# The W stage of a LoRA and routed-adapter kernel: another order of the weight pieces, a first piece in two transfers, PT in five parts over two queues

## The chip, the cores and the metric

One core of a Trainium2 chip (trn2) runs the kernel. The metric is the time on the device in microseconds, the median of several executions of the same program.

## The reference

```python
# x (8, 512, 2048), W (2048, 2048), lora_As (32, 2048, 16), lora_Bs (32, 16, 2048), all float32
base_out = jnp.einsum('bti,oi->bto', x, W) + b
lora_h   = jnp.einsum('bti,bir->btr', x, lora_As[adapter_mapping])      # one adapter per batch
lora_out = jnp.einsum('btr,bro->bto', lora_h, lora_Bs[adapter_mapping])
cond     = base_out + lora_out * 2
logits   = jnp.einsum('bsd,ed->bse', cond, route_w)                     # 8 experts, the top one
route_weight = one_hot(argmax(logits)) * max(logits)
h        = jnp.einsum('bsd,erd->bser', cond, A)                         # (8 experts x rank 16)
out      = x + jnp.einsum('bser,eor->bso', route_weight[..., None] * h, Bw)
```

The result `cond` is needed only in two products, with `A` and with `route_w`. So the kernel never makes it. It multiplies the weights together first and then works on x with the small product.

## The kernel before

The rows of `A` (128) and of `route_w` (8) stand beside each other as PT, 136 columns, cut into 16 chunks of 128 output features of W. All arrays are laid out so by the host.

**W stage.** It computes M = W^T PT, 2048 x 136. W comes in 32 pieces of 512 KB: 8 blocks of 256 input features (`NWB`), each in 4 parts along the output features (`NWH`), with 4 chunks to a part. A piece is 8 matmuls of 136 columns in float32, and the profile records each of them as two. SP loads the pieces into a ring of 8 (`w_ring`); from the ninth on it waits until PE has used the slot (L211). Pieces go block after block: block 0 parts 0 to 3, then block 1, and so on. A block has two accumulators, both in one of two double banks of PSUM (`bank_out`), used in turn. PT comes in 4 parts, each issued by SP just before one of the first four W pieces (L228 to L232); behind piece 4 SP issues the bias.

When a block is complete (`t_w` counts the pieces that PE has finished), ACT copies it from PSUM: the 128 columns rounded to `m_hi`, and the 8 routing columns twice to `ext`. DVE then subtracts to get the rest `m_lo` (`m_block` in each). The semaphore `v_m` counts DVE's lots, and PE waits for it before it writes the bank again (L502).

ACT's program during this stage is one loop over the 8 blocks. In the pass for block 1, ahead of that block's eviction and behind block 0's, it issues the eight loads of loraB (one adapter for each batch, 128 KB each) and two of loraA (L320 to L324); the rows' numbers were read much earlier. POOL waits for all eight, rearranges them into `lb_cols` and signals `g_lb` (L283, L284).

**The side products.** PE's program is written out in order: warm-up matmuls (L513 to L515), W pieces 0 to 19, then a wait for `g_lb` and the product of the loraB columns with PT (L519 to L523), the bias product (L527, which needs the chain of 16 operations in DVE over PT and the bias, L395 to L399), pieces 20 to 23, small products (L533, L536), pieces 24 to 31.

**The rest.** Then come eight batches of 512 tokens, the last in two halves. For each, PE computes the LoRA and routing product (L573), the main product in three passes of split float32 (L588 to L590), the routing (L598, L604, L615), and the output products of the batch before (L555 to L557). DVE adds x to them, and SP stores. x comes in 32 pieces of 1 MB; SP issues the first four within the W stage, behind pieces 19, 23, 27 and 31, and BwT (1 MB) behind piece 19 too.

Of the kernel before, what the change touches and what calls it, by code (L numbers as in the profile page):

```python
# [41 lines left out]
P = 128  # L42
# [4 lines left out]
def adaln_ffn(nc, xT, slot_of, W, PT, bias, loraA, loraB, BwT, outT):  # L47
    NB, NQ, _, PC, T = xT.shape
    C = NQ * PC
    NP2 = C // 2  # L50
    NWB, NWH, _, WO, WI = W.shape
    E = 8
    R = 16
    ER = E * R
    PN = ER + E
# [3 lines left out]
    BIAS_ROW = E + R  # L59
    XRING = 12  # L60
    WRING = 8
    NPT = 4
    SRING = 4
    NWP = NWB * NWH
    NPIECES = NB * NQ
    assert ER == P and WI == 2 * P and NWB == NP2 and NB * R == P and BIAS_ROW < GROUP

    ctx = ExitStack()
    with ctx:
# [6 lines left out]
        def sem(name):  # L76
            return ctx.enter_context(nc.semaphore(name))
# [3 lines left out]
        w_ring = sb("w_ring", [P, WRING, WO, WI], F32, phase1)  # L81
# [15 lines left out]
        pt = sb("pt", [P, C, PN], F32, phase1)  # L97
# [14 lines left out]
        m_hi = sb("m_hi", [P, C, ER], F32R)  # L112
# [34 lines left out]

        d_slots, d_bias, d_bw, d_lb, d_la0, d_la = (sem(n) for n in ("d_slots", "d_bias", "d_bw", "d_lb", "d_la0", "d_la"))
        d_pt = [sem(f"d_pt{i}") for i in range(NPT)]
        d_w = [sem(f"d_w{i}") for i in range(WRING)]  # L150
        d_x = [sem(f"d_x{i}") for i in range(XRING)]
        d_out = [sem(f"d_out{i}") for i in range(XRING)]
# [28 lines left out]
            return x_ring[:, k % XRING, 2 * j % PC:2 * j % PC + 2, t0:t0 + nt]  # L181

        CONSTS = E + 7
        WARM_UP = 9
        BW_AT = 19
        BP_AT, G_AT = 20, 24

        CHOOSE_AT, EHI_AT, ELO_AT = 1, 5, 3

        def out_banks(u, j):  # L190

# [15 lines left out]
        @block.sync  # L207
        def _(sp):
            def load_w(n):
                if n >= WRING:  # L210
                    sp.wait_ge(t_w, n - WRING + 1)  # L211
                sp.dma_start(w_ring[:, n % WRING, :, :], W[n // NWH, n % NWH]).then_inc(d_w[n % WRING], 16)

            def load_x(k):
                slot = k % XRING
                if k >= XRING:
                    sp.wait_ge(d_out[slot], 16 * (k // XRING))
                elif slot in EARLY:
                    sp.wait_ge(t_g, len(g_banks))
                    sp.wait_ge(v_bw, 1)  # L220
                sp.dma_start(x_ring[:, slot, :, :], xT[k // NQ, k % NQ]).then_inc(d_x[slot], 16)

            def store(k):
                sp.wait_ge(v_out, (k + 1) * (PC // 2))
                sp.dma_start(outT[k // NQ, k % NQ], x_ring[:, k % XRING, :, :]).then_inc(d_out[k % XRING], 16)


            for n in range(NWP):  # L228
                if n < NPT:
                    part = slice(n * C // NPT, (n + 1) * C // NPT)  # L230
                    sp.dma_start(pt[:, part, :], PT[:, part, :]).then_inc(d_pt[n], 16)
                load_w(n)  # L232
                if n == NPT:
                    sp.dma_start(bias_sb[:, :], bias).then_inc(d_bias, 16)
                if n == BW_AT:
                    sp.dma_start(bw_raw, BwT).then_inc(d_bw, 16)
                if n >= NWP - 4 * NQ and n % 4 == 3:
                    load_x((n - NWP + 4 * NQ) // 4)
            for k in range(NQ, XRING):
                load_x(k)  # L240
            LAG = 2
            LAST = NPIECES - NQ
            for k in range(LAST):
                store(k)
                if k >= LAG and k - LAG + XRING < NPIECES:
                    load_x(k - LAG + XRING)
            for u in range(NB - 1, NU):
                b, t0, nt = UNITS[u]
                for j in range(NP2):
                    sp.wait_ge(v_out, NP2 * u + j + 1)  # L250
                    q, c = 2 * j // PC, 2 * j % PC
                    sp.dma_start(outT[b, q, :, c:c + 2, t0:t0 + nt], x_pair(u, j)).then_inc(d_last, 16)
            for s in range(XRING):
                sp.wait_ge(d_out[s], 16 * len(range(s, LAST, XRING)))
            sp.wait_ge(d_last, 16 * NP2 * (NU - NB + 1))
# [39 lines left out]
        @block.scalar  # L295
        def _(act):

            act.dma_start(slots[:, :], slot_of).then_inc(d_slots, 16)
            act.wait_ge(d_slots, 16)
            slot = [act.value_load(slots[0:1, b:b + 1], min_val=0, max_val=NSLOTS - 1) for b in range(NB)]  # L300
# [7 lines left out]
            def copy(out, in_, done):  # L308
                act.activation(out, in_, ACT.Copy).then_inc(done, 1)  # L309

            def m_block(n):

                act.wait_ge(t_w, NWH * (n + 1))
                copy(m_hi[:, 2 * n:2 * n + 2, :], bank_out[n % 2][:, :, 0:ER], a_m)
                for i in range(2):
                    copy(ext[i][:, 2 * n:2 * n + 2, 0:E], bank_out[n % 2][:, :, ER:PN], a_m)

            act.wait_ge(g_const, CONSTS)
            for n in range(NWB):
# [60 lines left out]
        def _(dve):  # L380
            def sub(out, a, b, done):
                dve.tensor_tensor(out, a, b, ALU.subtract).then_inc(done, 1)  # L382

            def m_block(n):
                dve.wait_ge(a_m, 3 * (n + 1))
                sub(m_lo[:, 2 * n:2 * n + 2, :], bank_out[n % 2][:, :, 0:ER], m_hi[:, 2 * n:2 * n + 2, :], v_m)

            dve.memset(warm[:, :], 0.0).then_inc(v_warm, 1)

            dve.wait_ge(d_bias, 16)  # L390
            for c in range(C):
                if c % (C // NPT) == 0:
                    dve.wait_ge(d_pt[c // (C // NPT)], 16)
                if c == 0:
                    dve.tensor_scalar(pb_sum[0][:, :], pt[:, 0, :], bias_sb[:, 0:1], None, ALU.mult).then_inc(v_pb, 1)  # L395
                else:
                    dve.wait_ge(v_pb, c)
                    dve.scalar_tensor_tensor(out=pb_sum[c % 2][:, :], in0=pt[:, c, :], scalar=bias_sb[:, c:c + 1],
                                             in1=pb_sum[(c - 1) % 2][:, :], op0=ALU.mult, op1=ALU.add).then_inc(v_pb, 1)  # L399
# [94 lines left out]
        def _(pe):  # L494
            mm = pe.matmul

            def w_piece(n):

                blk, half = divmod(n, NWH)
                pe.wait_ge(d_w[n % WRING], 16 * (n // WRING + 1))  # L500
                if half == 0 and blk >= 2:
                    pe.wait_ge(v_m, blk - 1)  # L502
                for i in range(2):
                    for o in range(WO):
                        k = half * WO + o
                        if blk == 0 and i == 0 and k % (C // NPT) == 0:
                            pe.wait_ge(d_pt[k // (C // NPT)], 16)
                        last = mm(bank_out[blk % 2][:, i, 0:PN], w_ring[:, n % WRING, o, i * P:(i + 1) * P],  # L508
                                  pt[:, k, :], start=(k == 0), stop=(k == C - 1))
                last.then_inc(t_w, 1)  # L510


# [4 lines left out]
                w_piece(n)  # L517

            pe.wait_ge(g_lb, 1)  # L519
            for c in range(C):  # L520
                last = mm(bank_l[:, 0:PN], lb_cols[:, c, :, :].rearrange("p b r -> p (b r)"), pt[:, c, :],  # L521
                          start=(c == 0), stop=(c == C - 1))
# [18 lines left out]
            def out_pair(u, j):  # L541
                nt = UNITS[u][2]
                if u == 0 and j < 2:
                    pe.wait_ge(v_m, NWB)
                else:
                    pe.wait_ge(v_out, pairs_added(u, j))
                if u == 0 and j == 0:
                    pe.wait_ge(v_bw, 1)
                if j == 0:
                    pe.wait_ge(v_whlo, u + 1)  # L550
                hi, lo = wh_hi[u % 2][:, 0:nt], wh_lo[u % 2][:, 0:nt]
                for i in range(2):
                    o = slice((2 * j + i) * P, (2 * j + i + 1) * P)
                    out = out_banks(u, j)[:, i, :]
                    mm(out, bw_hi[:, o], hi, start=True, stop=False)  # L555
                    mm(out, bw_hi[:, o], lo, start=False, stop=False)  # L556
                    last = mm(out, bw_lo[:, o], hi, start=False, stop=True)  # L557
                last.then_inc(t_out, 1)

            pe.wait_ge(v_glo, 1)  # L560
            for u, (b, _, nt) in enumerate(UNITS):
# [4 lines left out]
                for r in range(C // NGROUPS):  # L566
                    for g in range(NGROUPS):
                        c = r * NGROUPS + g
                        if c % PC == 0:
                            x_landed(pe, NQ * b + c // PC)  # L570
                        if u == 0 and c % 2 == 0:
                            pe.wait_ge(a_m, 3 * (c // 2 + 1))
                        last = mm(bank_e[g * GROUP:(g + 1) * GROUP, 0:nt], ext[u % 2][:, c, :], x_pair(u, c // 2)[:, c % 2, :],  # L573
                                  start=(r == 0), stop=(r == C // NGROUPS - 1))
                last.then_inc(t_ext, 1)

                if u >= 1:
                    pe.wait_ge(a_h, u)
                else:
                    pe.wait_ge(v_m, NWB)  # L580
                h = bank_h[:, 0:nt]
                for j in range(NP2):
                    g = NP2 * u + j
# [71 lines left out]
```

## Time and profile before

| | us |
|---|---|
| median of 3 runs | 304.76 |
| lowest, highest | 304.1, 304.79 |
| span of the profiled execution | 302.6 |
| the profiled execution's own time on the device | not given beside its span |
| TensorE (PE) busy, matmul | 295.9 |
| VectorE (DVE) busy | 193.1 |
| ScalarE (ACT) busy | 99.0 |
| GpSimd (POOL) busy | 11.0 |

The span runs from the first to the last instruction of one execution. Busy time is the time in which an engine's rows lie, idle time the rest. PEld is TensorE's weight load, which overlaps its matmuls. Queues of DMA issues have a q behind the engine's name. The chain of waits is followed from the last instruction back to what released it, step by step. The granted clock (PEclk) of 1.00 stands for 2.4 GHz.

### The profile page before, as it was taken

Reading aid. Unit: us, or ns where it says so; the run is one execution under the profiler, and the core shown is the slowest. Engines: PE = TensorE matmul, PEld = TensorE weight load, DVE = VectorE, ACT = ScalarE, POOL = GpSimd, SP = SyncE. Lnnn points to the kernel's source line nnn. Section 1 sums busy time; section 2 is a strip of 40 time slices with the busy share of each in tenths; the row PEclk is TensorE's granted clock in tenths of the full one; section 3 lists DMA queues with packets and bytes.
Section 4 is the critical chain, followed back from the end, with each engine's and each line's share of the span. In section 5 each row is a group of like instructions: output and inputs, shape, how many; then the busy total and the mean of one; then the engine's idle time right before and its main releaser. Section 6 shows DMA issues by size and latency. Waiting matters only on the chain.

```text
span 302.6 us, 4629 instructions
## 1 busy us (share of the span) xinstructions
PE 295.9 (98%) x1857; PEld 233.5 (77%) x1857; DVE 193.1 (64%) x258; ACT 99.0 (33%) x147; POOL 11.0 (4%) x37
## 2 busy tenths in 40 slices
PE   7899999999999999999999999999999999999994
PEld 4899999997675885788488758866884787787994
DVE  0160000242894997498579839984985796698775
ACT  0020000223874332534253433424342533322410
POOL 6000300000100000000000000000000000000000
PEclk9999999999999999999999999999999999999999
DMA  7999999999920067739946991998399569536468
GB/s 245 400 404 394 415 412 411 414 417 418 421 107 2 25 252 259 298 133 388 418 172 237 417 405 54 379 395 337 118 377 417 202 220 406 208 151 266 178 218 299
DMA packets 20790, 88.44 MB, mean 292 GB/s; under 512 B 2210, under 2 KB 8354, under 8 KB 12962
## 3 DMA queue, kind: packets, MB, share of 16 engines
q1 hardware_dynamic: 18464, 86.06, 72.4%
q10 hardware_dynamic: 2306, 2.10, 2.0%
q8 instruction: 14, 0.23, 0.3%
q14 instruction: 6, 0.05, 0.0%
HBM read 54.60 MB, written 33.55 MB: 291 GB/s over the span
## 4 chain that ended last, share of the span: by engine, by line
PE 92%; DMA 3%; DVE 3%; SPq 1%; issue 0%
PE bank_out L508 18%; PE bank_h L588 11%; PE bank_h L590 10%; PE bank_h L589 10%; PE bank_e L573 9%; PE bank_out L555 9%; PE bank_out L557 9%; PE bank_out L556 9%; DMA w_ring<-W 3%; DVE x_ring L465 2%; PE bank_l L521 1%; PE bank_r L615 1%; PE bank_l L598 1%; PE bank_h L608 1%; PE bank_h L610 1%; PE bank_h L609 1%
## 5 line engine op out<-in xcount | busy, mean ns | idle before, releaser
L382 DVE TENSOR_TENSOR x_lo<-x_ring,x_hi 128x1024 fp32r<-128x1024 f32 (+1 forms) x72 | 78.9, 1106 | 41.1 <-ACT x_hi L309 41.1
L309 ACT ACTIVATE x_hi<-x_ring 128x1024 fp32r<-128x1024 f32 (+1 forms) x72 | 69.2, 966 | 85.8 <-PE bank_h L590 85.8
L465 DVE TENSOR_TENSOR x_ring<-bank_out,x_ring 128x1024 f32<-128x1024 f32 (+1 forms) x72 | 79.2, 1102 | 1.4 <-PE bank_out L557 1.1
L508 PE MATMUL bank_out<-pt,w_ring 128*128 128x136 f32 x512 | 60.6, 280 | 1.4 <-DMA w_ring<-W 1.4
L508 PEld LDWEIGHTS bank_out<-pt,w_ring 128*128 128x128 f32 x512 | 59.7, 190 | 2.8 <-DMA w_ring<-W 2.5
L588 PE MATMUL bank_h<-x_hi,m_hi 128*128 128x512 f32 (+1 forms) x144 | 55.1, 383 | 0.0
L555 PE MATMUL bank_out<-wh_hi,bw_hi 128*128 128x512 f32 (+1 forms) x144 | 54.6, 379 | 0.0
L590 PE MATMUL bank_h<-x_hi,m_lo 128*128 128x512 f32 (+1 forms) x144 | 53.3, 370 | 0.0
L556 PE MATMUL bank_out<-wh_lo,bw_hi 128*128 128x512 f32 (+1 forms) x144 | 53.2, 369 | 0.0
L557 PE MATMUL bank_out<-wh_hi,bw_lo 128*128 128x512 f32 (+1 forms) x144 | 53.2, 369 | 0.0
L589 PE MATMUL bank_h<-x_lo,m_hi 128*128 128x512 f32 (+1 forms) x144 | 53.1, 369 | 0.0
L588 PEld LDWEIGHTS bank_h<-x_hi,m_hi 128*128 128x128 f32 x144 | 27.0, 188 | 13.2 <-issue 8.5
L590 PEld LDWEIGHTS bank_h<-x_hi,m_lo 128*128 128x128 f32 x144 | 27.1, 188 | 5.0
L557 PEld LDWEIGHTS bank_out<-wh_hi,bw_lo 128*128 128x128 f32 x144 | 27.1, 188 | 5.0
L555 PEld LDWEIGHTS bank_out<-wh_hi,bw_hi 128*128 128x128 f32 x144 | 27.1, 188 | 4.8
L589 PEld LDWEIGHTS bank_h<-x_lo,m_hi 128*128 128x128 f32 x144 | 27.1, 188 | 4.6
L382 DVE TENSOR_TENSOR m_lo<-bank_out,m_hi 128x256 fp32r<-128x256 f32 x8 | 3.4, 424 | 42.5 <-ACT ext L309 42.5
L556 PEld LDWEIGHTS bank_out<-wh_lo,bw_hi 128*128 128x128 f32 x144 | 27.1, 188 | 4.2
L573 PE MATMUL bank_e<-x_ring,ext 128*32 128x512 f32 (+1 forms) x288 | 29.4, 548 | 0.0
L573 PEld LDWEIGHTS bank_e<-x_ring,ext 128*32 128x32 f32 x288 | 8.4, 109 | 16.4 <-issue 15.3
L309 ACT ACTIVATE m_hi<-bank_out 128x256 fp32r<-128x256 f32 x8 | 3.1, 383 | 44.4 <-PE bank_out L508 44.4
L356 ACT ACTIVATE e_sb<-bank_e,e_bias 128x512 f32<-128x512 f32 (+1 forms) x9 | 5.8, 642 | 25.9 <-PE bank_e L573 25.9
(77 smaller groups left out, 130.1 us busy)
## 6 DMA issues: line engine op xcount, KB each, us to landing
x_ring<-xT SPq DMA_DIRECT2D x32, 1024.0 KB, 9.0
outT<-x_ring SPq DMA_DIRECT2D x28, 1024.0 KB, 5.3
w_ring<-W SPq DMA_DIRECT2D x32, 512.0 KB, 9.0
outT<-x_ring SPq DMA_DIRECT2D x16, 256.0 KB, 2.4
pt<-PT SPq DMA_DIRECT2D x4, 272.0 KB, 5.8
x_ring<-loraB ACTq DMA_DIRECT2D x8, 128.0 KB, 10.6
la<-loraA ACTq DMA_DIRECT2D x8, 128.0 KB, 14.3
x_ring<-BwT SPq DMA_DIRECT2D x1, 1024.0 KB, 10.4
```

What stands on the lines that cost most here:

```text
L309: act.activation(out, in_, ACT.Copy).then_inc(done, 1)
L356: act.activation(e_sb[:, 0:nt], bank_e[:, 0:nt], ACT.Identity, bias=e_bias[:, 0:1]).then_inc(a_e, 1)
L382: dve.tensor_tensor(out, a, b, ALU.subtract).then_inc(done, 1)
L465: dve.tensor_tensor(x, out_banks(u, j), x, ALU.add).then_inc(v_out, 1)
L508: last = mm(bank_out[blk % 2][:, i, 0:PN], w_ring[:, n % WRING, o, i * P:(i + 1) * P], pt[:, k, :], start=(k == 0), stop=(k == C - 1))
L555: mm(out, bw_hi[:, o], hi, start=True, stop=False)
L556: mm(out, bw_hi[:, o], lo, start=False, stop=False)
L557: last = mm(out, bw_lo[:, o], hi, start=False, stop=True)
L573: last = mm(bank_e[g * GROUP:(g + 1) * GROUP, 0:nt], ext[u % 2][:, c, :], x_pair(u, c // 2)[:, c % 2, :], start=(r == 0), stop=(r == C // ...
L588: mm(h, m_hi[:, c, :], hi, start=(c == 0), stop=False)
L589: mm(h, m_hi[:, c, :], lo, start=False, stop=False)
L590: last = mm(h, m_lo[:, c, :], hi, start=False, stop=False)
```

## The change

The order of the W pieces is a list now. The first 16 pieces are the parts 0 of blocks 0 to 3, then their parts 1, and so on; pieces 16 to 31 are blocks 4 to 7 one after the other, as before. Four blocks are open at once, so block 2 accumulates in `bank_e` and `bank_h` and block 3 in `bank_r` and `bank_l`; these two are drained in two lots each, which makes 10 lots. Piece 0 comes in two transfers of two chunks each. PT comes in five parts (2, 2, 4, 4, 4 chunks), the first two issued by ACT ahead of all else, the other three by SP behind pieces 1, 3 and 5. The bias is issued behind piece 7. PE does 6 warm-up matmuls. ACT's and DVE's `m_block` wait for the piece that completes the block, and PE waits before L521 for the drain of the first four blocks. ACT's loop around `m_block` is as before.

```diff
+    PT_PARTS = [(0, 2), (2, 4), (4, 8), (8, 12), (12, 16)]
+    NPT = len(PT_PARTS)
+    OPEN = NWB // 2
+    ORDER = [(blk, part) for part in range(NWH) for blk in range(OPEN)] + [
+        (blk, part) for blk in range(OPEN, NWB) for part in range(NWH)]
+    DONE = [max(n for n in range(NWP) if ORDER[n][0] == blk) + 1 for blk in range(NWB)]
...
-        WARM_UP = 9
+        WARM_UP = 6
...
+        def w_banks(blk):
+
+            if blk == 2:
+                return [(bank_e, 4, 1), (bank_h, 5, 1)]
+            if blk == 3:
+                return [(bank_r, 6, 1), (bank_l, 7, 1)]
+            return [(bank_out[blk % 2], 2 * blk, 2)]
+
+        M_LOTS = [sum(len(w_banks(b)) for b in range(blk + 1)) for blk in range(NWB)]
...
-                sp.dma_start(w_ring[:, n % WRING, :, :], W[n // NWH, n % NWH]).then_inc(d_w[n % WRING], 16)
+                blk, part = ORDER[n]
+                if n == 0:
+                    sp.dma_start(w_ring[:, 0, 0:WO // 2, :], W[blk, part, :, 0:WO // 2, :]).then_inc(d_w_first, 16)
+                    sp.dma_start(w_ring[:, 0, WO // 2:WO, :], W[blk, part, :, WO // 2:WO, :]).then_inc(d_w[0], 16)
+                else:
+                    sp.dma_start(w_ring[:, n % WRING, :, :], W[blk, part]).then_inc(d_w[n % WRING], 16)
...
             for n in range(NWP):
-                if n < NPT:
-                    part = slice(n * C // NPT, (n + 1) * C // NPT)
-                    sp.dma_start(pt[:, part, :], PT[:, part, :]).then_inc(d_pt[n], 16)
                 load_w(n)
-                if n == NPT:
+                if n in (1, 3, 5):
+                    k = 2 + n // 2
+                    c0, c1 = PT_PARTS[k]
+                    sp.dma_start(pt[:, c0:c1, :], PT[:, c0:c1, :]).then_inc(d_pt[k], 16)
+                if n == 7:
                     sp.dma_start(bias_sb[:, :], bias).then_inc(d_bias, 16)
...
         def _(act):
 
+            for k in range(2):
+                c0, c1 = PT_PARTS[k]
+                act.dma_start(pt[:, c0:c1, :], PT[:, c0:c1, :]).then_inc(d_pt[k], 16)
             act.dma_start(slots[:, :], slot_of).then_inc(d_slots, 16)
...
             def m_block(n):
 
-                act.wait_ge(t_w, NWH * (n + 1))
-                copy(m_hi[:, 2 * n:2 * n + 2, :], bank_out[n % 2][:, :, 0:ER], a_m)
-                for i in range(2):
-                    copy(ext[i][:, 2 * n:2 * n + 2, 0:E], bank_out[n % 2][:, :, ER:PN], a_m)
+                act.wait_ge(t_w, DONE[n])
+                for bank, c, k in w_banks(n):
+                    sums = bank[:, :, 0:PN] if k == 2 else bank[:, 0:PN].unsqueeze(1)
+                    copy(m_hi[:, c:c + k, :], sums[:, :, 0:ER], a_m)
+                    for i in range(2):
+                        copy(ext[i][:, c:c + k, 0:E], sums[:, :, ER:PN], a_m)
...
-                blk, half = divmod(n, NWH)
-                pe.wait_ge(d_w[n % WRING], 16 * (n // WRING + 1))
-                if half == 0 and blk >= 2:
-                    pe.wait_ge(v_m, blk - 1)
...
+                blk, part = ORDER[n]
+                if part == 0 and blk >= OPEN:
+                    pe.wait_ge(v_m, M_LOTS[blk - OPEN if blk < OPEN + 2 else blk - 2])
+                halves = ((0, WO // 2), (WO // 2, WO)) if n == 0 else ((0, WO),)
...
             pe.wait_ge(g_lb, 1)
+            pe.wait_ge(v_m, M_LOTS[OPEN - 1])
```

DVE's `m_block` and the later waits for evicted blocks count in lots in the same way.

## Rows read from the trace of the kernel before

**Rows 1.** The page: busy time and share per engine, then the chain of waits.

```profile
PE 295.9 (98%) x1857; PEld 233.5 (77%) x1857; DVE 193.1 (64%) x258; ACT 99.0 (33%) x147; POOL 11.0 (4%) x37
...
PE 92%; DMA 3%; DVE 3%; SPq 1%; issue 0%
PE bank_out L508 18%; PE bank_h L588 11%; PE bank_h L590 10%; PE bank_h L589 10%; PE bank_e L573 9%; PE bank_out L555 9%; PE bank_out L557 9%; PE bank_out L556 9%; DMA w_ring<-W 3%; DVE x_ring L465 2%; PE bank_l L521 1%; PE bank_r L615 1%; PE bank_l L598 1%; PE bank_h L608 1%; PE bank_h L610 1%; PE bank_h L609 1%
```

**Rows 2.** Timeline of PE: start us, length us, line, operation, records, idle before.

```profile
1.19 3.87 PE L515 MATMUL bank_h<-warm 128*128 128x512 bf16 x9 [1.19 <-DVE warm L388]
4.97 2.12 PE L508 MATMUL bank_out<-pt,w_ring 128*128 128x136 f32 x16
8.29 4.06 PE L508 MATMUL bank_out<-pt,w_ring 128*128 128x136 f32 x32 [1.20 <-DMA w_ring<-W]
12.57 31.77 PE L508 MATMUL bank_out<-pt,w_ring 128*128 128x136 f32 x272 [0.23 <-DMA w_ring<-W]
44.18 3.87 PE L521 MATMUL bank_l<-pt,x_ring 128*128 128x136 f32 x32
```

**Rows 3.** Windows of the opening: length, busy per engine, granted clock, DMA share, GB/s.

```profile
0.00:4.00 4.00, 2.81 (x7) 1.01 (x8) 0.27 (x1) 0.00 (x0) 3.44 (x22) 1.00 0.55 182
4.00:8.00 4.00, 3.09 (x19) 2.07 (x17) 0.00 (x0) 0.00 (x0) 1.36 (x6) 1.00 0.98 324
8.00:12.00 4.00, 3.71 (x31) 3.69 (x32) 0.00 (x0) 0.00 (x0) 0.00 (x0) 1.00 1.01 390
12.00:16.00 4.00, 3.77 (x32) 3.57 (x32) 1.73 (x5) 1.22 (x1) 0.00 (x0) 1.00 1.02 412
```

**Rows 4.** Timeline of ACT and its DMA queue (ACTq), around block 0's eviction.

```profile
14.78 1.28 ACT L309 ACT_TABLE_LOAD   x1 [14.78 <-PE bank_out L508]
15.04 0.88 ACTq L322 DMA_DIRECT2D x_ring<-loraB  x2
16.07 0.38 ACT L309 ACTIVATE m_hi<-bank_out 128x256 fp32r<-128x256 f32 x1
...
16.57 3.34 ACTq L322 DMA_DIRECT2D x_ring<-loraB  x5
20.00 0.88 ACTq L304 DMA_DIRECT2D la<-loraA  x2
```

**Rows 5.** The loraB loads' line: issues, and times to landing.

```profile
L322 ACTq DMA_DIRECT2D x_ring<-loraB x8: 339/340/1322, 15.0 to 19.6; - x8
...
DMA to landing us min/median/max: 6.6/10.6/13.7
```

**Rows 6.** Timeline of POOL: the copy that makes the loraB columns.

```profile
33.29 1.89 POOL L284 COPY x_ring<-x_ring 128x2048 f32<-128x2048 f32 x1 [27.93 <-DMA x_ring<-loraB]
```

**Rows 7.** Timeline of SP's DMA queue: issues of W, BwT and x.

```profile
1.19 0.42 SPq L212 DMA_DIRECT2D w_ring<-W  x1
...
29.92 0.43 SPq L236 DMA_DIRECT2D x_ring<-BwT  x1
30.40 0.44 SPq L221 DMA_DIRECT2D x_ring<-xT  x1
```

**Rows 8.** DMA queues, q1 of SP, q10 of ACT: 20 to 33, then 63 to 74 us.

```profile
q1 hardware_dynamic: 1123, 4.10, 80.1%
q10 hardware_dynamic: 1125, 1.02, 23.3%
...
q1 hardware_dynamic: 556, 4.07, 88.3%
q10 hardware_dynamic: 558, 0.51, 13.5%
```

**Rows 9.** Windows at the end of the trace.

```profile
298.00:300.00 2.00, 0.51 (x5) 0.30 (x3) 1.22 (x2) 0.00 (x0) 0.00 (x0) 1.00 1.04 347
300.00:302.00 2.00, 0.00 (x0) 0.00 (x0) 0.00 (x0) 0.00 (x0) 0.00 (x0) 0.94 0.86 286
302.00:302.60 0.60, 0.00 (x0) 0.00 (x0) 0.00 (x0) 0.00 (x0) 0.00 (x0) 0.50 0.00 0
```

More of the change, by code:

```diff
@@ L61, in adaln_ffn @@
     WRING = 8
-    NPT = 4
     SRING = 4
     NWP = NWB * NWH
+    PT_PARTS = [(0, 2), (2, 4), (4, 8), (8, 12), (12, 16)]
[4 more added lines that the diff above has]
+    DONE = [max(n for n in range(NWP) if ORDER[n][0] == blk) + 1 for blk in range(NWB)]
     NPIECES = NB * NQ
@@ L149, in adaln_ffn @@
         d_pt = [sem(f"d_pt{i}") for i in range(NPT)]
+        d_w_first = sem("d_w_first")
         d_w = [sem(f"d_w{i}") for i in range(WRING)]
@@ L384, in m_block @@
             def m_block(n):
-                dve.wait_ge(a_m, 3 * (n + 1))
-                sub(m_lo[:, 2 * n:2 * n + 2, :], bank_out[n % 2][:, :, 0:ER], m_hi[:, 2 * n:2 * n + 2, :], v_m)
+                for i, (bank, c, k) in enumerate(w_banks(n)):
+                    sums = bank[:, :, 0:PN] if k == 2 else bank[:, 0:PN].unsqueeze(1)
+                    dve.wait_ge(a_m, 3 * (M_LOTS[n] - len(w_banks(n)) + i + 1))
+                    sub(m_lo[:, c:c + k, :], sums[:, :, 0:ER], m_hi[:, c:c + k, :], v_m)
             dve.memset(warm[:, :], 0.0).then_inc(v_warm, 1)
@@ L391, in _ @@
             for c in range(C):
-                if c % (C // NPT) == 0:
-                    dve.wait_ge(d_pt[c // (C // NPT)], 16)
+                for k in range(NPT):
+                    if c == PT_PARTS[k][0]:
+                        dve.wait_ge(d_pt[k], 16)
                 if c == 0:
@@ L497, in w_piece @@
             def w_piece(n):
-                blk, half = divmod(n, NWH)
-                pe.wait_ge(d_w[n % WRING], 16 * (n // WRING + 1))
-                if half == 0 and blk >= 2:
-                    pe.wait_ge(v_m, blk - 1)
[L503 to L509, printed above, removed]
+                blk, part = ORDER[n]
+                if part == 0 and blk >= OPEN:
+                    pe.wait_ge(v_m, M_LOTS[blk - OPEN if blk < OPEN + 2 else blk - 2])
+                halves = ((0, WO // 2), (WO // 2, WO)) if n == 0 else ((0, WO),)
+                for o0, o1 in halves:
+                    if o1 == WO:
+                        pe.wait_ge(d_w[n % WRING], 16 * (n // WRING + 1))
+                    else:
+                        pe.wait_ge(d_w_first, 16)
+                    for i in range(2):
+                        bank = w_banks(blk)[i][0][:, 0:PN] if len(w_banks(blk)) == 2 else w_banks(blk)[0][0][:, i, 0:PN]
+                        for o in range(o0, o1):
+                            k = part * WO + o
+                            for p in range(NPT):
+                                if blk == 0 and i == 0 and k == PT_PARTS[p][0]:
+                                    pe.wait_ge(d_pt[p], 16)
+                            last = mm(bank, w_ring[:, n % WRING, o, i * P:(i + 1) * P],
+                                      pt[:, k, :], start=(k == 0), stop=(k == C - 1))
                 last.then_inc(t_w, 1)
@@ L543, in out_pair @@
                 if u == 0 and j < 2:
-                    pe.wait_ge(v_m, NWB)
+                    pe.wait_ge(v_m, M_LOTS[-1])
                 else:
@@ L571, in _ @@
                         if u == 0 and c % 2 == 0:
-                            pe.wait_ge(a_m, 3 * (c // 2 + 1))
+                            pe.wait_ge(a_m, 3 * M_LOTS[c // 2])
                         last = mm(bank_e[g * GROUP:(g + 1) * GROUP, 0:nt], ext[u % 2][:, c, :], x_pair(u, c // 2)[:, c % 2, :],
@@ L579, in _ @@
                 else:
-                    pe.wait_ge(v_m, NWB)
+                    pe.wait_ge(v_m, M_LOTS[-1])
                 h = bank_h[:, 0:nt]
```

## The prediction

> **What bounds the kernel now.** I read the page first. TensorE (PE) is busy for 98% of the span and carries 92% of the chain of waits, DMA 3% [rows 1]. So two kinds of change can move the end: one that lets PE start sooner or pause less, and one that makes PE pause where it doesn't now. The timeline of PE says where its pauses are [rows 2]. The weight pieces (16 recorded matmuls each) start at 4.97 us, pause until 8.29, pause shortly (the 32 matmuls from 8.29 take 4.06) and run without a gap from 12.57 to 44.18, where the product with the loraB columns (L521) starts. These are 17 pieces in 31.61 us, 1.86 each. Everything behind them is dense as well. Had the first three pieces run without a pause from 4.97, the fourth would start at 10.55 and not at 12.57: the pauses of the opening are worth 2.0 us, and an earlier first piece perhaps one more. That is all the change can win, about 3 us.
>
> Next come the things that PE waits for in this stage. DMA runs at full share there; the stretches of 4 us moved 182, 324, 390 and 412 GB/s, so 0.73 MB had moved at 4 us, 2.02 at 8, 3.58 at 12 and 5.23 at 16 [rows 3]. Then I looked at who issues the loraB loads, since L521 needs them: ACT does, behind the eviction of block 0. ACT was released at 14.78, the end of the fourth piece, and the first loraB load went out 0.26 us later, at 15.04 [rows 4]. They had landed when POOL started its copy at 33.29, and the copy took 1.89 [rows 5, 6]. PE came to L521 at 44.18, so the loraB columns were ready 9.0 us before they were needed. That slack is the most important number of this case.
>
> **The opening.** The change asks for fewer bytes ahead of each early piece. W is 0.524 MB a piece, PT 0.278 MB a quarter. I take from before how far the moved bytes ran ahead of those that a piece needed when it could start: at 4.97 us 1.04 MB had moved for 0.80 needed, at 8.29 2.14 for 1.61, at 12.57 3.82 for 3.21 [rows 2, 3]. So the surplus is 0.24, then 0.53, then 0.61 MB, and I keep it.
> - First half piece with PT 0: 0.40 needed, 0.64 moved, at about 3.8 us. Six warm-ups instead of nine end at 1.19 + 6 x 0.43 = 3.75 us, so PE has work nearly throughout. The warm-ups run at 0.43 us for 512 columns, which is 1.2 GHz, and the first pieces at 2.4 GHz, so the clock rose by 4.97 us, after 3.8 us of work (the clock column says 1.00 there all the same [rows 3]; I go by the pace [rows 2]). The early half piece is computed partly at 1.2 GHz and ends near 5.3.
> - Second half with PT 1: 0.80 needed, about 5.0 us. Piece 0 is done near 6.2.
> - Piece 1 (1.33 needed, 1.86 moved): 7.5 us. It ends at 9.4. Piece 2 stands behind PT part 2 (2.13 needed, 2.68 moved): 9.7 us, ends 11.55. Piece 3 (2.65, 3.23): 11.1 us, hence it starts at 11.55 when PE is free.
> - Pieces 4, 5, 6 are there at 13.2, 14.4 and 16.4 us, PE wants them at 13.4, 15.3 and 17.1. No more pauses.
> So piece 3 starts at 11.55 instead of 12.57: **1.0 us gained**. Bounds: nothing, if the narrower rows (PT parts of two chunks, W in halves) or the 270 to 350 GB/s of this phase eat it, even 0.5 lost if the clock rises late because the warm-up is shorter; 3.0, if PE starts at 3.8 and never pauses. The three warm-ups taken away (1.3 us) were beside a DMA wait and are worth nothing by themselves.
>
> The change also puts two PT parts on ACT's queue. SP saves two issues of about 0.43 us [rows 7] ahead of the later pieces, which are held by bytes and not by issues, so I count nothing. ACT's slot loads start 0.9 us later; ACT idles until 14.78 anyway. The Trainium skill, "DMA: Bandwidth & Descriptors", section "Issuing engines are not separate DMA queues", says that issuing from several engines saves only the sequencer's time; by that rule the second queue brings no bandwidth, as counted. Were it wrong and the first 0.40 MB came 0.5 us sooner, the gain would still be cut down to 1.0 by piece 1.
>
> **What the opening moves.** Four blocks now finish with pieces 12, 13, 14 and 15, instead of block 0 with piece 3. Block 0's eviction in ACT waits for 13 pieces. Piece 12 ended before at 12.57 + 10 x 1.86 = 31.2, after at 30.2. Behind this wait in ACT's program stand the eight loraB loads and two loraA loads, the lot that goes out when block 1's turn comes. The diff doesn't move them. So the first loraB load goes out at 30.2 + 0.26 = **30.4 us instead of 15.04**, 15.4 later, with a slack of 9.0.
>
> How long do they take? Before, first issue to last landing was 15.04 to 33.2 (19.6 + 13.7 us of landing gives 33.3): 18.2 us [rows 4, 5]. It is so slow because SP's queue is full: from 20 to 33 us the two queues moved the same number of packets, 1123 and 1125, W rows of 4 KB against loraB rows of 1 KB, and loraB had 1.02 MB in 13 us, 78 GB/s. Beside rows of 8 KB (the x pieces, 63 to 74 us) the small queue had 0.51 MB in 11 us, 46 GB/s [rows 8]. Of the 18.2 us, 1.05 MB / 78 = 13.4 are the move, 4.8 lead and landing.
> Now SP's side at the new time. SP issues W 19, BwT (1 MB) and x piece 0 (1 MB) in a row when PE has finished piece 11; before, the last two at 29.9 and 30.4 us [rows 7], after, 1.0 earlier. So 2.6 MB stand right before the loraB loads, where before three W pieces stood (1.6 MB). Then W 20 to 23, x piece 1, W 24, 25. One of the loraB loads (0.131 MB) goes beside x piece 1 at 46 and not 78 GB/s: 1.2 us more. If all eight find W rows and the lead is the old one, 18.2 us; with x piece 1, 19.4; with the longer lead as well, 2.6 MB at 0.41 against 1.6, up to 2.4 more, 21.8. I take 19.4, near the row of the same transfer. The loads land at 49.8, POOL's copy of 1.89 us and its two hand-overs make it 51.8. Lower bound: the queue beside them nearly empty; then they take their issue time of 4.9 us plus some 6.6 (the shortest landing [rows 5]), 41.9, and PE gets the columns at 43.9. Upper bound: all at 46 GB/s, 22.8 + 4.8 = 27.6 us, PE gets them at 60.0.
>
> PE reaches L521 at 44.2 - 1.0 = 43.2. It waits there 8.6 us, and L521 starts at 51.8 instead of 44.2: **7.6 us lost net, the opening's gain already in it**. The gain doesn't vanish: it lets piece 12 end earlier, and so the loads go out earlier.
> Behind this wait stands the whole rest of PE's program, in order: L521, the bias product, pieces 20 to 31 and the 8 batches. SP's W issues wait for PE in turn, but W 20 to 27 are in the ring by then, so PE finds them.
>
> **The clock after the wait.** Before, PE paused 1.20 us at most and went on at 2.4 GHz. At the end of the trace PE works until 298.5, and the granted clock is 0.94 on the mean of 300 to 302 and 0.50 after that: half speed for the last 0.24 us of that window, so it fell near 301.8, 3.3 us after the last matmul [rows 9]. A pause of 8.6 us should bring it to 1.2 GHz. In the opening it took 3.8 us of matmuls until the clock was up; at half speed that costs **1.8 us** (bounds: 0, if it stays up or the pause is short; 2.7). The Trainium skill, "TensorE: Matmul & The Clock Gate", Part 1, says that an idle PE falls back to half rate and that the default is throttled; by that rule the 1.8 us are due, without it they aren't.
>
> **Smaller things.** PE waits for six m_lo lots before L521 (all four blocks drained, two of them in two lots each). ACT's ten issues take 5.9 us before (15.04 to 20.9, one held for 1.3 [rows 4]), so blocks 1 to 3 drain from some 37 us on; five lots of about 0.7 us (m_hi 0.38 [rows 4] and two small copies) end near 41. That is before 43.2 by 2 us, and the loraB wait covers it: nothing. If there were no loraB wait and the issues were held for 4 us more, it would cost about 2. Pieces 16, 20, 24 and 28 wait for lots drained some pieces before: nothing. Bias is issued later and the pb_sum chain runs in an idle DVE, ahead of a product behind L521: nothing. After L521 no wait of before had any slack to give back, PE is dense; x pieces come from a DMA queue that gains on PE during the stall. So nothing returns.
>
> **Sum.** Span of the profiled execution 302.6, + 7.6 + 1.8 = 312.0. The median of the runs shown is 304.76, 2.2 above that span; no time of the profiled execution itself is given, so I add these 2.2: **314.2 us**.
>
> **Rivals.**
> 1. The loraB loads come in time and only the opening counts, or the issue isn't held at all: 304.8 - 1.0 = 303.8, down to 301.8 with the whole 3.0. This is the other side. It needs the last landing by 41.2, that is 10.8 us after the first issue. For it: SP's queue is nearly drained by 28 us, since W alone asks for 0.524 / 1.86 = 282 GB/s. Against it: BwT and x piece 0 are issued just ahead, and the trace's 18.2 us. It decides below 10.8 us. Chance 5%.
> 2. The wait is there but PE's clock stays up or the loads are some 2 us faster: 302.6 + 7.6 + 2.2 = 312.4, to 310.4 with faster loads. For it: the clock didn't fall in any pause inside this trace. Chance 22%.
> 3. The loads go at the 8 KB rows' pace, because BwT and x 0 and 1 are all beside them, or the longer lead holds: 2 to 8 us more, 316.5 to 322. For it: 46 GB/s in [rows 8]; against: most of SP's queue after x 0 is W. Chance 15%.
> 4. The change does nothing to the time (the gain of an unbroken opening and a short wait cancel): 304.8. Needs the landing at just 12.8 us. Chance 2%.
> My forecast, with its own range of 312.8 to 316, has 56%.
>
> Range at 8 in 10: low 309.5 (no clock loss, loads 3 us faster), high 317.5. Within 0.3% (0.9 us) is what a measurement of this kernel can't tell from no change. Faster 0.05, same 0.02, slower 0.93.
>
> **What the profile of the changed kernel would show.** The first W matmul at 3.8 us, piece 3 at about 11.5, pieces at 1.86 us without a gap from there. The first loraB issue near 30.4 us on ACT, POOL's copy starting near 49.8, a gap of PE of some 8 us ahead of L521 whose releaser is the POOL copy. After it, matmuls of L521 starting 0.23 us apart instead of 0.12 for some 3.5 us. From W piece 20 on, the distances of before. I am wrong if POOL's copy ends before 43 us, if the gap is there but something after it gives time back, or if the opening still pauses at piece 1 as long as before.

## The result, and the profile after

| | before | changed |
|---|---|---|
| median, us | 304.77 (4 runs, 304.1 to 304.92) | 316.96 (4 runs, 316.01 to 318.95) |
| profiled execution, span, us | 302.6 | 314.0 (316.01 on the device) |
| mean granted clock | 0.999 | 0.984 |

The changed kernel is slower by 4.2%: the ratio is 1.0417, 95% interval 1.0377 to 1.0458. The forecast was 314.2 us, range 309.5 to 317.5. All ratios in this document leave out executions over 1.5% above the fastest of their kernel; only e4 below has such, three of ten.

The page of the changed kernel first: busy time, the granted clock in 40 slices of 7.85 us, the chain by engine.

```profile
PE 297.7 (95%) x1854; PEld 235.9 (75%) x1854; DVE 193.4 (62%) x260; ACT 99.1 (32%) x153; POOL 10.4 (3%) x37
...
PEclk9999995799999999999999999999999999999999
...
PE 88%; DMA 7%; DVE 1%; ACTq 1%; POOL 1%; issue 0%; SPq 0%; ACT 0%
```

PE is busy 95% of a longer span, and DMA has 7% of the chain instead of 3% [rows 1]. The clock row has two weak slices, the seventh and eighth, at 47 to 63 us. That is the place to look at. The timeline of PE there and in the opening (weight pieces are L545 now, the loraB product is L559):

```profile
1.19 2.74 PE L552 MATMUL bank_h<-warm 128*128 128x512 bf16 x6 [1.19 <-DVE warm L417]
4.61 2.17 PE L545 MATMUL bank_out<-pt,w_ring 128*128 128x136 f32 x16 [0.68 <-DMA pt<-PT]
7.25 2.12 PE L545 MATMUL bank_out<-pt,w_ring 128*128 128x136 f32 x16 [0.47 <-DMA w_ring<-W]
9.20 1.19 PE L545 MATMUL bank_e<-pt,w_ring 128*128 128x136 f32 x8
...
11.16 1.09 PE L545 MATMUL bank_r<-pt,w_ring 128*128 128x136 f32 x8
...
13.02 3.87 PE L545 MATMUL bank_out<-pt,w_ring 128*128 128x136 f32 x32
...
35.26 7.58 PE L545 MATMUL bank_out<-pt,w_ring 128*128 128x136 f32 x64
52.74 6.74 PE L559 MATMUL bank_l<-pt,x_ring 128*128 128x136 f32 x32 [9.91 <-POOL x_ring L306]
...
59.73 7.68 PE L545 MATMUL bank_out<-pt,w_ring 128*128 128x136 f32 x64
```

Line by line against [rows 2]: the first piece starts at 4.61 instead of 4.97, piece 3 (in `bank_r`) at 11.16 instead of 12.57. That is the opening's gain, 1.4 us. Then the pieces run without a gap to 42.8. And then PE stands for 9.91 us, released by POOL. The product starts at 52.74 instead of 44.18, **8.56 us later**, and lasts from 52.74 to 59.41, 6.67 us, against 3.80 from 44.18 to 47.98, **2.87 more**. Together 11.43. The span grew by 11.4. All that is behind it takes its old time.

Who was late? ACT and its queue (the loraB issues are L349), then the loads' landings, then POOL's copy:

```profile
29.94 1.28 ACT L334 ACT_TABLE_LOAD   x1 [29.94 <-PE bank_out L545]
30.21 1.22 ACTq L349 DMA_DIRECT2D x_ring<-loraB  x2
...
34.60 1.17 ACTq L329 DMA_DIRECT2D la<-loraA  x2
35.81 0.38 ACT L334 ACTIVATE m_hi<-bank_out 128x256 fp32r<-128x256 f32 x1 [4.04 <-PE bank_l L545]
```

```profile
L349 ACTq DMA_DIRECT2D x_ring<-loraB x8: 339/364/685, 30.2 to 34.1; - x8
...
DMA to landing us min/median/max: 7.4/11.4/16.6
```

```profile
50.80 1.89 POOL L306 COPY x_ring<-x_ring 128x2048 f32<-128x2048 f32 x1 [45.42 <-DMA x_ring<-loraB]
```

Against [rows 4 to 6]: ACT was released at 29.94 instead of 14.78, the first loraB load went out at 30.21 instead of 15.04, the last landed at 50.7 (34.1 + 16.6). The three lines are the same work, shifted by 15 us, and 2.3 us slower on the way (20.6 from first issue to the copy's start, 18.25 before).

Where do the 2.3 us come from? Not from the lead: the first packet of these loads moved 3.5 us after the first issue in both traces, at 18.5 us before and at 33.7 now. ACT's DMA queue (q10; packets, MB, share) of the changed kernel from 33.7 to 36.7, from 36.7 to 42.7 and from 42.7 to 47 us:

```profile
q10 hardware_dynamic: 145, 0.14, 13.3%
...
q10 hardware_dynamic: 510, 0.47, 23.0%
...
q10 hardware_dynamic: 274, 0.25, 17.1%
```

In the middle almost only W rows of 4 KB are beside it, and it moves 78 GB/s, the pace of [rows 8]. In the first and the third stretch many rows of 8 KB are there (BwT and x piece 0, then x piece 1), and it moves 47 and 58 GB/s. These 0.39 MB took 7.3 us; at 78 GB/s they would have taken 5.0. That is the 2.3 us.

Block 1 is drained at 35.81, when the issues are out. That eviction is in nobody's way.

The granted clock, in the column behind POOL's, around the pause:

```profile
46.00:48.00 2.00, 0.00 (x0) 0.00 (x0) 0.00 (x0) 0.00 (x0) 0.00 (x0) 1.00 1.00 387
48.00:50.00 2.00, 0.00 (x0) 0.00 (x0) 0.00 (x0) 0.00 (x0) 0.00 (x0) 0.55 1.05 401
56.00:58.00 2.00, 2.00 (x11) 2.00 (x10) 0.00 (x0) 0.00 (x0) 0.00 (x0) 0.50 0.03 12
58.00:60.00 2.00, 2.00 (x15) 1.63 (x14) 0.00 (x0) 0.44 (x2) 0.00 (x0) 0.89 0.00 0
```

It falls near 48.2 (0.55 in 48 to 50), 5.4 us after the last piece, and is back near 58.4 (0.89 in 58 to 60), 5.7 us after PE started again. All of the product up to then is at 1.2 GHz.

### The profile page after: what moved, and what is told of

It reads as the page before. It is cut to its first block, busy times and chain, and to the rows that moved or that the text cites. A ratio compares the mean times of both kernels' runs of the same rounds, so it can differ in the third digit from the quotient of the medians.

```text
span 314.0 us, 4634 instructions
## 1 busy us (share of the span) xinstructions
PE 297.7 (95%) x1854; PEld 235.9 (75%) x1854; DVE 193.4 (62%) x260; ACT 99.1 (32%) x153; POOL 10.4 (3%) x37
## 4 chain that ended last, share of the span: by engine, by line
PE 88%; DMA 7%; DVE 1%; ACTq 1%; POOL 1%; issue 0%; SPq 0%; ACT 0%
PE bank_out L545 11%; PE bank_h L626 11%; PE bank_h L628 10%; PE bank_h L627 10%; PE bank_out L593 9%; PE bank_out L595 9%; PE bank_out L594 9%; PE bank_e L611 9%; DMA x_ring<-loraB 5%; PE bank_l L559 2%; DMA w_ring<-W 2%; PE bank_r L653 1%; DVE x_ring L495 1%; PE bank_l L636 1%; ACTq L349 1%; PE bank_e L545 1%
## 5 line engine op out<-in xcount | busy, mean ns | idle before, releaser
L545 PE MATMUL bank_out<-pt,w_ring 128*128 128x136 f32 x384 | 46.1, 280 | 1.1 <-DMA pt<-PT 0.7
L545 PEld LDWEIGHTS bank_out<-pt,w_ring 128*128 128x128 f32 x384 | 45.1, 190 | 2.5 <-DMA w_ring<-W 2.2
L409 DVE TENSOR_TENSOR m_lo<-bank_out,m_hi 128x256 fp32r<-128x256 f32 x6 | 2.5, 425 | 49.7 <-ACT ext L334 49.7
L559 PE MATMUL bank_l<-pt,x_ring 128*128 128x136 f32 x32 | 6.7, 400 | 9.9 <-POOL x_ring L306 9.9
L559 PEld LDWEIGHTS bank_l<-pt,x_ring 128*128 128x128 f32 x32 | 6.5, 302 | 10.1 <-POOL x_ring L306 10.1
## 6 DMA issues: line engine op xcount, KB each, us to landing
x_ring<-loraB ACTq DMA_DIRECT2D x8, 128.0 KB, 11.4
```

Of the source, the lines that this page charges most:

```text
L545: last = mm(bank, w_ring[:, n % WRING, o, i * P:(i + 1) * P], pt[:, k, :], start=(k == 0), stop=(k == C - 1))
```

## The experiments

Theory: the loraB loads are issued behind an eviction that waits for piece 12, and this alone makes the loss. Rival A: the new order costs something by itself (drains in a row, the wait for six lots). Rival B: the longer product isn't the clock. Rival C: the loads are slow by themselves, not by what stands beside them. Times of different chips are compared through the kernel before that ran beside them.

**e1: the changed kernel, loads at their old time.**

```diff
-                if n == 1:
+                if n == 0:
+                    act.wait_ge(t_w, 4)
                     for b in range(NB):
                         act.dma_start(lb[:, b, :, :]...
```

> The changed kernel, with ACT issuing the eight loraB and two loraA loads where they went out before the change: after the fourth piece (t_w at 4), ahead of block 0's eviction. If the loss is the loads issued 15 us later, the wait ahead of the loraB product goes and with it the half-speed clock behind it; the opening's 1.5 us (fourth piece at 11.05 instead of 12.57) is what is left: 303.3 us. If the new order itself costs something (four blocks drained in a row, the wait for six lots, more accumulators), the time stays above 306.

Measured 302.95 us, ratio 0.9937 (0.9916 to 0.9958). The pause ahead of the product is gone, as its timeline of PE shows:

```profile
4.27 5.19 PE L546 MATMUL bank_out<-pt,w_ring 128*128 128x136 f32 x32 [0.34 <-DMA pt<-PT]
...
42.72 3.87 PE L560 MATMUL bank_l<-pt,x_ring 128*128 128x136 f32 x32
```

The product starts at 42.72, 10.0 us earlier than in the changed kernel and 1.5 earlier than before. Rival A falls: with the loads on time the new order costs nothing here.

**e2: the kernel before, loads late.**

```diff
-                if n == 1:
+                if n == 3:
+                    act.wait_ge(t_w, 13)
```

> The kernel before, with the ten loads issued after 13 pieces (in the pass for block 3) instead of after block 0. Nothing else is changed. If the late issue alone makes the loss: first load at 31.4 us, landed some 20.6 later as in the changed kernel, loraB product at 54 instead of 44.2, 2.9 more for the clock: 317.5 us. If the loss needs the new order, 304.8.

Measured 318.38 us, ratio 1.0448 (1.0395 to 1.05). PE's timeline (pieces are L509, the product L522):

```profile
8.38 35.67 PE L509 MATMUL bank_out<-pt,w_ring 128*128 128x136 f32 x304 [1.38 <-DMA w_ring<-W]
54.09 6.57 PE L522 MATMUL bank_l<-pt,x_ring 128*128 128x136 f32 x32 [10.04 <-POOL x_ring L284]
```

The same pause and the same slow product in the old order. With e1 this shows the cause from both sides.

**e4: only W beside the late loads.** BwT goes out behind piece 27, the x pieces behind all of W.

```diff
-        BW_AT = 19
+        BW_AT = 27
...
-                if n >= NWP - 4 * NQ and n % 4 == 3:
-                    load_x((n - NWP + 4 * NQ) // 4)
-            for k in range(NQ, XRING):
+            for k in range(XRING):
                 load_x(k)
```

> The changed kernel with BwT issued behind piece 27 instead of 19 and the first four x pieces behind all W pieces, so that only W stands in SP's queue beside the late loraB loads. If the loads are slow by what stands beside them, W asks for 282 of some 410 GB/s, the rest carries 1.05 MB in 8.2 us: landed near 41, product at 43 to 44, time 303.5 to 305. If they are slow by themselves (rows of 1 KB at 78 GB/s, 13.4 us and 4.8 of lead), they land at 48.5, product at 50.5, and with the clock's loss 314 us.

Measured 305.59 us over ten executions, from 303.23 to 310.88; the ratio, without the three above 308, is 0.9979 (0.9953 to 1.0006). The median misses the expected 303.5 to 305. In the profiled execution (306.65) the columns came 2.05 us late. The three slowest weren't profiled, and what held them is not shown. DMA queues of e4, 31 to 42 us, then of the changed kernel, 31 to 50 us (packets, MB, share):

```profile
q1 hardware_dynamic: 688, 2.52, 60.8%
q10 hardware_dynamic: 1373, 1.25, 37.8%
```

```profile
q1 hardware_dynamic: 1382, 6.58, 86.1%
q10 hardware_dynamic: 1189, 1.09, 16.9%
```

With less in SP's queue, ACT's moved 1.25 MB in 11 us (114 GB/s), in the changed kernel 1.09 MB in 19 us (57 GB/s, the wait for the first packet included). POOL's copy started at 42.65, 12.7 us after the first issue instead of 20.6. Rival C falls: the late issue cost so much since 2.1 MB of BwT and x, and then another x piece, share the DMA engines with it. The last load landed at 42.6, 1.6 later than the expected 41.

The short pause taught something else. PE's product and the clock of e4:

```profile
44.59 5.64 PE L557 MATMUL bank_l<-pt,x_ring 128*128 128x136 f32 x32 [2.05 <-POOL x_ring L304]
```

```profile
42.00:44.00 2.00, 0.55 (x5) 0.34 (x3) 0.42 (x1) 0.54 (x3) 1.35 (x1) 1.00 1.04 420
44.00:46.00 2.00, 1.41 (x8) 1.41 (x9) 0.00 (x0) 0.00 (x0) 0.71 (x2) 0.75 1.02 418
46.00:48.00 2.00, 2.00 (x10) 2.00 (x10) 0.00 (x0) 0.00 (x0) 0.58 (x2) 0.50 1.06 440
```

After a pause of 2.05 us the clock went to half speed, and it did so when PE was back at work (0.75 in 44 to 46 puts the fall near 45.0; 0.50 in 46 to 48). The product took 5.58 us, so 2.05 us of waiting cost 3.8.

**e3 and g1, g2: is the longer product the clock?** e3 is the changed kernel with 44 matmuls in the pause whose result isn't used; its edit stands here. g1 is the changed kernel with `WARM_UP = 9`, g2 is g1 with 52 such matmuls in the pause.

```diff
-            pe.wait_ge(g_lb, 1)
             pe.wait_ge(v_m, M_LOTS[OPEN - 1])
+            for _ in range(44):
+                mm(bank_h[:, :], warm[:, 0:P], warm[:, :], start=True, stop=True)
+            pe.wait_ge(g_lb, 1)
```

> The changed kernel with 44 matmuls of 512 columns on the idle accumulator between the drain wait and the wait for the loraB columns (44 x 0.216 = 9.5 us, which fills the pause of 9.9). They compute nothing that is used. If 2.9 us of the loss are the half-speed clock after the pause, the loraB product's 32 matmuls take 3.8 us instead of 6.7 and the time falls by 2.9, to 313.5 to 314. If the clock isn't the cause of the longer product (its operands, say), it stays at 316 to 317.

Measured 317.21 us, ratio 1.0438 (1.0392 to 1.0484): no gain on the whole. PE's timeline:

```profile
4.71 6.15 PE L545 MATMUL bank_out<-pt,w_ring 128*128 128x136 f32 x32 [0.78 <-DMA pt<-PT]
...
44.06 9.66 PE L558 MATMUL bank_h<-warm 128*128 128x512 bf16 x44
55.00 3.97 PE L561 MATMUL bank_l<-pt,x_ring 128*128 128x136 f32 x32 [1.28 <-POOL x_ring L306]
```

The product is short again (55.00 to 58.91, with 32 matmuls at full pace), so rival B falls. But this execution lost nearly as much elsewhere: its first two pieces took from 4.71 to 10.9, since the clock rose only at 9.2 by the pace of the matmuls, and the loraB columns came 2.3 us later than in the changed kernel, 1.4 of it from the opening. The times decide nothing here, so the comparison was made again from a base with nine warm-ups.

> The changed kernel as it is (late loads) with nine warm-ups, base of the next run: 316.5 us, the wait of some 10 us ahead of the loraB product in it and that product at 6.7 us.

> g1_changed_nine_warmups with 52 matmuls that compute nothing used (52 x 0.216 = 11.2 us) between the drain wait and the wait for the loraB columns. e3_fill_the_wait kept the clock up, but its profiled run lost 1.4 us in the opening, where the clock rose at 9.2 us, and its loads landed 2.3 us later. With nine warm-ups the opening is the same in both kernels. If the clock's loss of 2.9 us is real in the time, 1.5 to 2.9 less than g1 (the filler may end up to 1.5 us behind the loads), 314 to 315. If the loads get slower by as much when PE works, no difference.

g1 315.56 us, ratio 1.0377 (1.0352 to 1.0403); g2 314.19 us, ratio 1.0326 (1.0305 to 1.0348). The product in g1, then the filler and the product in g2:

```profile
53.16 5.35 PE L559 MATMUL bank_l<-pt,x_ring 128*128 128x136 f32 x32 [10.07 <-POOL x_ring L306]
```

```profile
42.77 11.17 PE L558 MATMUL bank_h<-warm 128*128 128x512 bf16 x50
53.78 3.87 PE L561 MATMUL bank_l<-pt,x_ring 128*128 128x136 f32 x32
```

Filled, the kernel is 1.4 us faster. Its time lies where it was expected, the difference just under the 1.5 to 2.9, since g1 came out below its expected 316.5. In g1's profiled execution the clock was back 2.8 us after the restart, not 5.7 as in the changed kernel's, and the product took 5.3 us. So the clock costs 1.5 to 2.9 us, by when it comes back. It had fallen earlier, too:

```profile
44.00:46.00 2.00, 0.00 (x0) 0.00 (x0) 0.11 (x1) 0.00 (x0) 0.00 (x0) 0.94 1.05 419
```

This puts g1's fall near 45.8, 2.7 us after its last piece, and it was back at 56.0. In the changed kernel it fell at 48.2 and was back at 58.4, in e2 at 49.2 and 59.4: in all three it stood at half speed for 10.2 us. In these traces an earlier fall goes with an earlier return; why the fall comes 2.7 or 5.4 us after the last piece is not shown.

**The opening, with the loads on time.** Four kernels on one chip, then two on another; all are e1 with further edits.

```diff
f1, h0:  -        WARM_UP = 6
         +        WARM_UP = 9
f2 = f1: -  ACT: the two PT parts
         +  SP: PT 0, W first half, PT 1, W second half
f3 = f1: -    ORDER = part by part over four blocks
         +    ORDER = [(blk, part) for blk in range(NWB) for part in range(NWH)]
         +    PT parts 2, 3, 4 behind pieces 0, 1, 2
h1 = h0: -  piece 0 in two transfers and two waits
         +  piece 0 in one
```

> The same kernel as e1_loads_early, here as the base for the next three on one chip: 302.9 us, 1.8 below the kernel before.

> e1_loads_early with nine warm-up matmuls instead of six. Between executions with six, the clock rose at 3.8, 4.0, 6.8 and 9.2 us; with nine it should rise near 4.8 every time. The fourth piece is held by the bytes of W unless the clock comes as late as 9.2, so the median moves by less than 0.3 (302.9), with less scatter. Rival: PE's early start was worth something; nine warm-ups end at 5.06 and cost the 0.8 us by which the first piece comes sooner: 303.7.

> f1_nine_warmups with the first two PT parts issued by SP, each ahead of its half of piece 0, instead of by ACT. If bytes alone count, the first half lands within 0.3 us of before and nothing follows: 302.9. If the second queue brings bandwidth or issue time at the start, the first piece comes 0.5 to 1 us later and the time rises by at most that, 303.5.

> f1_nine_warmups with the W pieces again block after block, and the PT parts behind pieces 0, 1 and 2, since a block then needs all of PT by piece 3. Piece 0 in two transfers stays. If the order makes the gain, the fourth piece waits again for 3.21 MB instead of 2.65: it starts at 12.3 and the time is 304.3 to 304.7. If the split first piece makes it, 303.

> The same kernel as f1_nine_warmups, as the base of the next and for a second interval: 303.1 us, 1.1 to 1.2 below the kernel before.

> h0_nine_warmups_again with piece 0 in one transfer and one wait. PE is busy with warm-ups until 5.06 us and the second half of piece 0 had landed at 5.1, so the split buys nothing once nine warm-ups run: within 0.3 us of h0. If the split counts (narrower rows of 2 KB are slower or the earlier half feeds PE), 0.5 us or more to either side.

| kernel | median, us | ratio to before | 95% interval |
|---|---|---|---|
| e1, six warm-ups | 302.95 | 0.9937 | 0.9916 to 0.9958 |
| f0, the same kernel again | 304.55 | 0.9990 | 0.9974 to 1.0006 |
| f1, nine warm-ups | 303.15 | 0.9961 | 0.9947 to 0.9974 |
| h0, the same as f1 | 303.19 | 0.9956 | 0.9939 to 0.9974 |
| f2, PT on SP's queue alone | 304.51 | 0.9993 | 0.9978 to 1.0009 |
| f3, blocks in turn | 303.97 | 0.9984 | 0.9971 to 0.9997 |
| h1, piece 0 whole | 304.01 | 0.9991 | 0.9976 to 1.0007 |

f0 missed its expectation by 1.6 us although it is e1. The first pieces and the product in f0, then in f1:

```profile
5.04 6.39 PE L546 MATMUL bank_out<-pt,w_ring 128*128 128x136 f32 x32 [1.11 <-DMA pt<-PT]
...
44.62 3.87 PE L560 MATMUL bank_l<-pt,x_ring 128*128 128x136 f32 x32
```

```profile
5.00 4.64 PE L546 MATMUL bank_out<-pt,w_ring 128*128 128x136 f32 x32
...
42.83 3.87 PE L560 MATMUL bank_l<-pt,x_ring 128*128 128x136 f32 x32
```

Both start at 5.0; the first 32 matmuls take 6.39 us in f0, most of them at the pace of 1.2 GHz, and 4.64 in f1, and the product follows 1.8 us later. With six warm-ups PE stood for 1.11 us before the first piece and the clock rose at 10.0 us; with nine there was no pause, and it rose at 6.6. So the three warm-ups are worth 1.4 us on this chip, where f0's executions lay at 302.56 to 305.08 and f1's at 302.71 to 304.12. The prediction had them at nothing, and f1's expectation at less than 0.3. Nine don't fix the rise either: it was expected near 4.8 every time, and in the nine profiled executions with nine warm-ups it came between 3.9 and 6.6 us. Nor are six always slower: e1 beside its kernel before has the lowest ratio of the table, and its interval overlaps f1's.

f2: the second queue is worth 1.4 us, where at most 0.6 was expected. Its pieces, then the window 3 to 5 us of f2 and of f1 (last column GB/s):

```profile
4.79 1.09 PE L545 MATMUL bank_out<-pt,w_ring 128*128 128x136 f32 x8
6.21 1.19 PE L545 MATMUL bank_out<-pt,w_ring 128*128 128x136 f32 x8 [0.33 <-DMA w_ring<-W]
8.66 2.12 PE L545 MATMUL bank_out<-pt,w_ring 128*128 128x136 f32 x16 [1.26 <-DMA w_ring<-W]
```

```profile
3.00:5.00 2.00, 2.00 (x8) 0.87 (x7) 0.00 (x0) 0.00 (x0) 1.97 (x15) 1.00 0.92 207
```

```profile
3.00:5.00 2.00, 2.00 (x7) 0.81 (x5) 0.00 (x0) 0.00 (x0) 1.97 (x15) 1.00 1.07 357
```

From 3 to 5 us the rows of PT (1 KB) and of the W halves (2 KB) together move at 207 GB/s on one queue and at 357 on two. From 1 to 3 us one queue was ahead (165 against 124 GB/s); over 1 to 7 us it is 1.41 MB against 1.70, and piece 1 starts at 8.66 instead of 7.6. By the Trainium skill, "DMA: Bandwidth & Descriptors", section "Issuing engines are not separate DMA queues", a second queue saves issue time alone. Issue time is part of it here (SP's two further issues put W piece 1 back by 0.9 us), but the lower GB/s at full DMA share is not explained by it. The measurement decides. Which of the two counts more wasn't separated.

f3: the order, with the places of the PT parts that go with it, is worth 0.8 us (303.97 against 303.15), where 1.4 to 1.8 was expected. The fourth piece starts at 12.2 here: 10.25 and one piece more.

```profile
5.00 2.06 PE L545 MATMUL bank_out<-pt,w_ring 128*128 128x136 f32 x16
7.91 2.12 PE L545 MATMUL bank_out<-pt,w_ring 128*128 128x136 f32 x16 [0.84 <-DMA w_ring<-W]
10.25 11.45 PE L545 MATMUL bank_out<-pt,w_ring 128*128 128x136 f32 x96 [0.22 <-DMA w_ring<-W]
```

h1: the split first piece is worth 0.8 us too, where I had expected nothing. In its profiled execution, the slowest of 12, PE waits twice for PT in piece 0. Its pieces, and the window 7 to 9 us:

```profile
5.51 0.70 PE L543 MATMUL bank_out<-pt,w_ring 128*128 128x136 f32 x4 [0.86 <-DMA pt<-PT]
7.09 5.18 PE L543 MATMUL bank_out<-pt,w_ring 128*128 128x136 f32 x28 [0.87 <-DMA pt<-PT]
```

```profile
7.00:9.00 2.00, 1.91 (x9) 1.92 (x10) 0.00 (x0) 0.00 (x0) 0.00 (x0) 0.59 1.03 420
```

The whole W piece had landed at 5.2 us, about when the second half does otherwise, but PT part 1 came at 7.0 instead of 5.3. Beside W rows of 4 KB PT's queue got less of the engines than beside rows of 2 KB: from 3 to 5 us it moved 0.14 MB here and 0.22 in h0. After the second wait the clock fell as well (0.59), and piece 1 started at 9.7. The faster executions of h1 (303.9) were not profiled; how much of their 0.8 us is PT and how much the clock stays open.

## Why the prediction was right

- **The slack of 9.0 us against a shift of 15.4.** It held: the shift was 15.2. This step decides the case: e1 takes the shift away and the loss goes, e2 makes it in the old order and the loss comes.
- **The opening.** 1.0 us predicted, 1.4 measured. The first piece started at 4.61, not at 3.8, and that cost nothing, since piece 1 waited for W anyway. Piece 1 and piece 2 were in place at 7.25 and 9.20 instead of 7.5 and 9.7; DMA moved 377 GB/s at 5 to 7 us, where the kernel before had 312. Two parts were taken for free that aren't: the warm-ups (up to 1.8 us by the execution) and the second queue (1.4 us with its issue time). That the warm-ups didn't show is luck: in this execution the clock was up before the first piece (its 16 matmuls take 2.17 us), the earliest rise of the five with six warm-ups. In f0 it rose at 10.0 us, and the product came 0.4 us later than in the kernel before, about the lower bound of the prediction.
- **The loads' duration.** 19.4 us predicted, 20.5 measured. The longer lead that was left in the bounds didn't come: it was 3.5 us as before. What was too small is the term for the rows of 8 KB, 1.2 us for one load beside x piece 1; beside BwT and both x pieces it was 2.3.
- **L559's start.** 51.8 predicted, 52.74 measured: 7.6 against 8.56 us lost net.
- **The clock.** 1.8 us predicted, 2.87 in the profiled execution, above the bound of 2.7. The prediction took its way up from the opening (3.8 us of work), and e4 happens to fit that: back 3.8 us after the restart, 1.8 lost. After the long pauses it took 2.8, 5.3 and 5.7 us (g1, e2, the changed kernel). This is the term that was most off for its size.
- **Nothing comes back behind the product.** Right: +11.43 at piece 20, +11.4 at the end.
- **The sum.** The span was 314.0 and not 312.0: 0.9 by the product's start, 1.1 by the clock. From span to time on the device 2.2 us were added, 2.0 are right for this execution. It was the fastest of the four, and the median lies 0.95 above it. The other three had spans of 314.3, 316.0 and 317.1; what makes the last two longer stays open. Their mean clock is lower (0.978 against 0.984), but in e2 the execution at 0.978 had a span of 315.6 and one at 0.983 had 316.7, so this doesn't tell.

The median of 316.96 thus lies within the range but above the forecast's own 312.8 to 316, among the times of rival 3. Part of rival 3 did happen, the longer stretch beside rows of 8 KB, though it added 1.1 us and not 2 to 8. Rival 1 (loads in time) needed BwT and x out of the way: four of e4's ten executions lie at 303.2 to 303.6 us. Rival 4 has a slip, on which nothing rests: 44.2 less 2.0 and less 30.4 is 11.8 us, not 12.8.

The version to keep is f1: the change, the loads issued after piece 3, nine warm-ups. It beats the kernel before by 0.4%, 1.2 us in f1 and 1.4 in h0, and by the ratios the changed kernel takes 4.6% longer. Its advantage over six warm-ups is shown on one chip only.

## What to carry to other kernels

When work is reordered so that something finishes later, list everything that stands behind its wait in the same engine's program, its DMA issues too, and give each its slack against the shift. Transfers that aren't connected with the wait belong ahead of it, or behind a wait of their own. A pause of TensorE that brings its clock down costs more than its length: here 2.05 us became 3.8 and 9.9 became 12.8.

## What the runs showed of the hardware

- A pause of 2.05 us between matmuls brought the clock to half speed, some 0.4 us after PE had started again (e4), and two of 0.86 and 0.87 us in the opening did so in h1, 0.3 us after the second. Pauses of 1.20 [rows 2], 1.26 (f2), 1.28 (e3) and 1.38 us (e2) did not. The length of the pause alone doesn't decide it.
- When PE stood for long, the clock fell 2.7 (g1), 3.3 [rows 9], 5.1 (e2) and 5.4 us (changed kernel) after its last matmul.
- With six warm-ups the clock rose between 3.8 and 10.0 us in the five profiled executions, with nine between 3.9 and 6.6 in nine of them; the pace of the matmuls shows it, the clock column reads 1.00 there.
- DMA at a share of 0.92 to 1.07 moved 207 GB/s or 357 GB/s with rows of 1 and 2 KB on one queue or on two. Issue time is part of it; the rest is not explained.
- Rows of 1 KB on one queue got 78 GB/s beside rows of 4 KB on the other, 46 to 58 where rows of 8 KB were beside them, and 114 beside a queue that was partly empty.
